# High digit's one-hot from eight shifted copies of the digit and four comparisons of 2048 elements, in place of four copies and eight comparisons of 1024

## The reference

```python
s0 = jnp.einsum('bshq,eq->bshe', _l2norm(q0), _l2norm(keys0))
s1 = jnp.einsum('bshq,eq->bshe', _l2norm(q1), _l2norm(keys1))
sc0, ix0 = jax.lax.top_k(s0, K)
sc1, ix1 = jax.lax.top_k(s1, K)
cs = (sc0[..., :, None] + sc1[..., None, :]).reshape(b, s, H, K * K)
ci = (ix0[..., :, None] + ix1[..., None, :]).reshape(b, s, H, K * K)
fs, pos = jax.lax.top_k(cs, K)
fi = jnp.take_along_axis(ci, pos, axis=-1)
w = jax.nn.softmax(fs, axis=-1)
down = expert_down[fi]
up = expert_up[fi]
inner = jnp.einsum('bsd,bshkd->bshk', hidden_states, down)
act = jax.nn.gelu(inner, approximate=False)
out = jnp.einsum('bshk,bshko->bso', act * w, up)
```

## Time and profile before

| | |
|---|---|
| time of three runs | 1363.95, 1364.64, 1365.32 us; median 1364.64 |
| profiled execution | 1364.77 us; its span 1363.0 us |
| DVE busy | 1241.4 us (91%) |
| PE busy | 1012.5 us (74%) |
| POOL busy | 925.8 us (68%) |
| ACT busy | 901.4 us (66%) |
| granted TensorE clock, mean | 0.76 |

### The profile page before, as it was taken

One profiled execution on the slowest core, in us unless ns is written; L12 is line 12 of the kernel. 1 busy time (PEld: TensorE's weight loads), 2 busy tenths in 40 slices (PEclk: granted clock), 3 DMA queues, 4 the chain that ended last, 5 costly groups with the idle time before them and its releaser, 6 DMA issues.

```text
span 1363.0 us, 38569 instructions
## 1 busy us (share of the span) xinstructions
PE 1012.5 (74%) x9443; PEld 659.5 (48%) x9443; DVE 1241.4 (91%) x9666; ACT 901.4 (66%) x4045; POOL 925.8 (68%) x1881
## 2 busy tenths in 40 slices
PE   2746777877878877887888788788867878877644
PEld 1514454645445554644555464455635545453433
DVE  4529696999999999999999999999999999999994
ACT  1546857577686867768686776868577686857442
POOL 4336666685868768586876858677685867768561
PEclk8867777679787786878777787877688787776665
DMA  2010000000000000000000000000000000000000
GB/s 56 7 28 3 9 13 10 11 13 11 14 3 23 4 13 13 12 13 4 23 5 13 13 12 13 4 23 4 13 13 11 13 4 17 4 8 13 6 6 7
DMA packets 35682, 16.56 MB, mean 12 GB/s; under 512 B 15392, under 2 KB 35248, under 8 KB 35458
## 3 DMA queue, kind: packets, MB, share of 16 engines
q1 hardware_dynamic: 34834, 13.81, 4.2%
q10 hardware_dynamic: 624, 0.30, 0.1%
HBM read 7.58 MB, written 6.01 MB: 10 GB/s over the span
## 4 chain that ended last, share of the span: by engine, by line
DVE 49%; ACT 13%; PE 12%; POOL 12%; issue 10%; SPq 1%; DMA 1%; DVEq 0%; POOLq 0%; ACTq 0%
DVE idx L1549 12%; DVE val L1547 7%; DVE scores L1552 6%; DVE oh L1562 6%; DVE cr L1620 6%; PE banks L1135 3%; DVE best L1618 3%; DVE wl L1582 3%; ACT ns_junk L942 3%; DVE masked L1502 2%; ACT act_g L919 2%; ACT eh L997 2%; POOL ce L691 2%; POOL std L654 2%; PE bankQ L1236 2%
## 5 line engine op out<-in xcount | busy, mean ns | idle before, releaser
L1549 DVE FIND_INDEX8 idx<-val,scores 128x8 uint16<-128x64 f32 x1472 | 298.0, 242 | 0.1
L1547 DVE MAX8 val<-scores 128x8 f32<-128x64 f32 x1472 | 205.6, 230 | 0.2
L1300 PE MATMUL bankM<-wl,oh 128*128 128x16 f16 x5888 | 161.0, 172 | 56.4 <-DVE wl L1582 52.4
L665 POOL TENSOR_TENSOR qscale<-nmx,power 128x16 f32<-128x16 f32 x46 | 151.1, 3284 | 60.9 <-DVE nmx L1526 60.9
L1300 PEld LDWEIGHTS bankM<-wl,oh 128*128 128x128 f16 x5888 | 157.1, 101 | 71.6 <-DVE wl L1582 61.6
L1552 DVE MATCH_REPLACE8 scores<-val,scores 128x64 f32<-128x64 f32 x736 | 149.6, 233 | 0.0
L1562 DVE TENSOR_SCALAR oh<-eh 128x1024 f16<-128x1024 int16 x368 | 134.1, 429 | 12.6 <-ACT eh L997 12.3
L1549 DVE MATCH_VALUE_LOAD idx<-val,scores 128x8 f32 x1472 | 140.2, 95 | 0.0
L942 ACT ACTIVATE ns_junk<-bankQ 128x32 f32<-128x32 f32 x736 | 132.8, 269 | 5.2 <-PE bankQ L1253 5.1
L942 ACT ACTIVATION_READ_ACCUMULATOR ns_junk<-bankQ 128x1 f32 x736 | 133.1, 282 | 0.0
L979 ACT ACTIVATE wcell<-wn 128x400 f16<-128x400 f32 x46 | 24.9, 542 | 136.6 <-POOL wn L716 136.6
(11 more groups left out here) (199 smaller groups left out, 3033.5 us busy)
## 6 DMA issues: line engine op xcount, KB each, us to landing
h_in<-h_rows SPq DMA_DIRECT2D x45, 64.0 KB, 2.7
out<-o_sb SPq DMA_DIRECT2D x45, 64.0 KB, 1.5
x_in<-in_x SPq DMA_DIRECT2D x16, 93.8 KB
x_in<-in_x SPq DMA_DIRECT2D x16, 62.5 KB
h_rows<-hsum SPq DMA_DIRECT2D x16, 62.0 KB
h_rows<-hsum SPq DMA_DIRECT2D x16, 61.0 KB
h_rows<-hsum SPq DMA_DIRECT2D x16, 60.5 KB
x_in<-in_x SPq DMA_DIRECT2D x16, 31.0 KB
```

The source lines that it names most:

```text
L665: g.tensor_tensor(qscale[c.slot(t)][:, :, :].rearrange("p h s -> p (h s)"), nmx[:, :, :].rearrange("p h s -> p (h s)"), power[0:QT, 0, :], ...
L1300: last = e.matmul(coef[:, g, :, :], oh[:, k, g, :, :].rearrange("p v t -> p (v t)"), wl[:, part, k, :, TG * g:TG * (g + 1)], start=k + par ...
L1547: last = v.max(out=v_[:, hd, s, best8], in_=src[:, hd, s, :])
L1549: last = v.max_index(out=i_[:, hd, s, best8], in_max=v_[:, hd, s, best8], in_values=src[:, hd, s, :])
```

## The change

`SHIFTS` is 8 in place of 4, and `VALUES`, the values of each copy, is 4 in place of 8.

```diff
@@ -20,7 +20,7 @@
 PAIRS = H // 2
 SLOTS = 32
 EH, EL, TG = 32, 4, 4
-SHIFTS = 4
+SHIFTS = 8
 VALUES = EH // SHIFTS
 QT = 128
 NQ = -(-B * T // QT)
```

## The result

| | before | after |
|---|---|---|
| median of the runs | 1364.88 us (1363.95 to 1365.32) | 1402.47 us (1401.38 to 1403.95) |
| profiled execution, its span | 1364.77, 1363.0 us | 1403.95, 1402.2 us |
| DVE, ACT busy | 1241.4, 901.4 us | 1229.6, 964.1 us |
| granted TensorE clock, mean | 0.76 | 0.766 |

The change makes the kernel slower: 1402.47 / 1364.88 = 1.0278, 95% interval 1.0266 to 1.0291. That is 37.6 us where 44 were forecast, and inside the range.

What follows compares the result with a forecast made beforehand. The prediction took the chain of waits, half DVE and half the other engines, as the bound. To 1364.8 us it added 43 for fourteen batches and 1.2 for the end, giving 1409 us, range 1385 to 1426.

Steps and rivals of the forecast that it cites:

- What bounds the kernel: Whole kernel: DVE has 49% of the chain, other engines the rest; about 20 of 46 copy sets lie on it.
- The price of a copy: On ACT: copies start 0.36 us apart, so four more cost 1.43 us a tile, 66 us in all.
- The saving on DVE: Comparisons: four of 2048 replacing eight save a fixed part of 0.065 us each, 0.26 a tile, 12 us in all.
- The batch's walk: Delay followed from tile 1 to the next tile 1: 3.1 us a batch, 43 us over fourteen three-tile batches.
- the sign that the walk gave for being wrong: On ACT: the walk is wrong if tile 2's copies come less than 1 us late.
- The other sign: On POOL: the walk is wrong if idle time at `nmx` or the next batch's squares shrinks with the delay.
- The first two batches: At the start: these batches have two tiles and more reserve, so nothing was counted for them.
- the term forecast for the end: Last tile's end, with no other work: 1.43 - 0.26 = 1.2 us added.
- The floor: Rival: only the 20 copy sets on the old chain count, less 7 us from comparisons: 1387 us; chance 0.2.
- The ceiling: Rival: all copies count in full, 66 us, and the comparisons give nothing back: 1431 us; chance 0.08.
- Faster: Rival: DVE sets the pace, ACT has room, and only the 12 us saved on DVE show: 1353 us; chance 0.05.
- No change: Rival: tile 2's reserve and DVE's gain eat the floor's 29 us, or the TensorE clock is granted higher; chance 0.04.

Runs made afterwards that it cites:

- dve_alone: The changed kernel with only the first four copies written per tile, the others zeroed once at the start, four comparisons of 2048 kept: 1352.92 us, ratio 0.9915.
- act_alone: The kernel before with four more copies per tile into a buffer nothing reads, ahead of the comparisons' signal; eight comparisons of 1024 stay: 1423.67 us, ratio 1.0438.
- many_t01: The kernel before with eight copies and four comparisons of 2048 in tiles 0 and 1, tile 2 as before: 1401.21 us, ratio 1.0276.
- many_t0: The kernel before with eight copies and four comparisons of 2048 in tile 0 of each batch alone: 1393.61 us, ratio 1.0214.
- spare_ahead: The kernel before with four copy-long activations on ACT in tile 0 alone, behind `wm` and ahead of convT, the norms and `hn`: 1395.08 us, ratio 1.0224.
- shifts2: The kernel before with two copies and sixteen comparisons of 512 per tile, in place of four and eight: 1394.83 us, ratio 1.0223.
- spare_behind: The kernel before with four copy-long activations on ACT in tile 0 alone, between `hn` and `hnT`: 1373.57 us, ratio 1.0064.
- act_behind: The kernel before with four copy-long activations on ACT behind `wm` in every tile, behind all three signals of `merged_weights`: 1383.97 us, ratio 1.0143.
- many_t1: The kernel before with eight copies and four comparisons of 2048 in tile 1 of each batch alone: 1377.57 us, ratio 1.0103.
- many_t2: The kernel before with eight copies and four comparisons of 2048 in tile 2 of each batch alone: 1365.44 us, ratio 1.0010.
- later4: The kernel before with tile 0's `merged_weights` behind `hn` on ACT, its DVE users behind two steps of tile 1's choosing, four copies: 1421.94 us, ratio 1.0418.
- later8: The same move as later4, with eight copies and four comparisons per tile: 1433.07 us, ratio 1.0498 against the kernel before.
- the kernels of the table: The kernel before, the changed kernel, and many_t2, many_t1, many_t0 and many_t01, with eight copies in some tiles only: medians 1364.88 to 1402.47 us.
- the two halves of the change: act_alone, the added copies without larger comparisons (+59.3 us), and dve_alone, the larger comparisons without added copies (-11.4 us).

## Why the prediction was right, and where its terms were off

**What bounds the kernel.** Right: the chain is shared by engines in the kernel before, and DVE's 96% did not hide the copies. dve_alone (-11.4) and act_alone (+59.3) show both sides of it.

**The price of a copy.** Right: 1.43 us for four, by the timeline. ACT's busy time rose by 62.7 us rather than 66.

**The saving on DVE.** Right: a mean of 697 ns, starts 0.60 apart, 11.8 us less busy, 11.4 us in dve_alone. By the distance of the starts the fixed part is 0.067, where 0.065 was forecast. The groups' busy time gives (134.1 - 120.4) / 184 = 0.074, as some comparisons of the kernel before take longer than 429 ns (six take some 0.6). The start of some 150 cycles that the Trainium skill gives every instruction ("VectorE: DVE Perf Modes", "Side-by-side: where the cycles go for N=2048 bf16"), with 29 us to gain, is not what the engine spends: the measured 11.8 decides.

**The batch's walk.** Right in its mechanism: ACT's copies went onto the chain in each batch, and the path led over tile 2's comparisons, PE, tile 0's copies, `hn` and the queries. Its size was off. It gave 3.1 us a batch, 43 over fourteen, and a batch costs 81.9 - 79.6 = 2.3.

The terms by tile: tile 2's copies were charged 1.43 less a reserve of 1.23, and all of 1.43 in every third batch. That reserve was spent in each batch (DVE begins 0.03 us after the last of them), but POOL's shorter `qscale` gave back more than what was left of the delay, where the walk had POOL take it over in full. With tiles 0 and 1 the time is +37.0, with all three +37.6. Tile 1 cost 13.4 / 16 = 0.84 a tile rather than 1.2, and tile 0 29.4 / 16 = 1.84 rather than 1.43.

The walk followed one batch, and a batch of the kernel before is not like the next one. From tile 1's first copy to tile 2's it took the 24.81 us of that batch; in the next one it is 26.00, and the mean of eleven is 25.55. After the change it is 26.00 each time. So the sign that the walk gave for being wrong, tile 2's copies less than 1 us late, came (0.46) by the mean and did not (1.19) by the batch followed. The other sign did not come: POOL's idle time at `nmx` went from 60.9 to 62.7 us and at the squares from 29.1 to 38.5.

**Luck in the size.** The distance of 81.9 is not the mark of this change. The changed kernel, many_t01, many_t0, spare_ahead and shifts2 all have it on average, from the third interval at the latest, with 12, 8 or 4 further activations a batch, or with DVE's work added in their place. In the changed kernel and many_t01 the granted clock falls and rises at the same places of every batch, in many_t0 and spare_ahead at the same places of every second one. That the clock's pattern holds the batches there is argued from this, not shown. If it is so, a walk that adds delays can't give the 2.3, and that it came within 0.8 of it is partly luck.

**The theory of two rounds.** The expectations rest on a later theory: the distance of the batches is the longer of two closed paths, A over the copies of all three tiles and B over tile 1's and tile 0's copies and VectorE between. It met many_t01 (1400 to 1407, measured 1401) and spare_behind (1372, measured 1374); spare_ahead was expected by many_t0's time (1385 to 1394, measured 1395). It missed act_alone by 13 us, act_behind by 18, many_t1 by 6, many_t0 by 9, many_t2 by 4, dve_alone by 4, shifts2 by 19, later4 by 71 and later8 by 44. So it is not a model of this kernel.

**The first two batches.** I counted nothing for them, for their reserve, and this step failed. In the timeline of DVE the tiles of those batches, and the first of three tiles, begin their comparisons at these times, before:

```profile
138.79 1.43 DVE L1562 TENSOR_SCALAR oh<-eh 128x1024 f16<-128x1024 int16 x4
...
163.38 1.44 DVE L1562 TENSOR_SCALAR oh<-eh 128x1024 f16<-128x1024 int16 x4 [2.57 <-ACT eh L997]
...
232.41 1.43 DVE L1562 TENSOR_SCALAR oh<-eh 128x1024 f16<-128x1024 int16 x4 [3.10 <-ACT eh L997]
...
276.79 1.42 DVE L1562 TENSOR_SCALAR oh<-eh 128x1024 f16<-128x1024 int16 x4
```

and after:

```profile
141.45 1.28 DVE L1562 TENSOR_SCALAR oh<-eh 128x2048 f16<-128x2048 int16 x2
...
168.97 1.30 DVE L1562 TENSOR_SCALAR oh<-eh 128x2048 f16<-128x2048 int16 x2 [4.46 <-ACT eh L997]
...
241.46 1.29 DVE L1562 TENSOR_SCALAR oh<-eh 128x2048 f16<-128x2048 int16 x2 [4.74 <-ACT eh L997]
...
285.60 1.29 DVE L1562 TENSOR_SCALAR oh<-eh 128x2048 f16<-128x2048 int16 x2
```

The delay is 2.7, 5.6, 9.1 and 8.8 us (6.3 in the tile left out after the second). DVE waited for the copies there already (2.57 and 3.10), and waits longer now. 2.0 us of it were there ahead of the first copy (137.10 after, 135.13 before). They are hardly the change's: in the kernels of the table the first copy begins at 134.8 to 137.3.

The sum as measured: 8.8 up to 276.79; then to the comparisons at 1284.2, which are at 1322.2 now, another 29.2 in 12.7 batches, 2.3 each; and a rest of 1.2, the term forecast for the end. That is 39.2, the difference of the two spans; the medians are 37.6 apart. So the forecast of 44 was near because too much a batch and too little at the start partly cancelled, which is luck as well.

**The rivals.** The floor (1387) fell: its 20 sets became 44, since a later ACT puts more of its copies on the chain. Its sentence that no reserve can bring it lower was not put to the test, as the time came out above. The ceiling (1431) fell, though what it was said to need came: tile 2's reserve was spent every time. Faster (1353) is what dve_alone shows, and would have needed copies at no cost. No change fell, and the mean granted clock hardly moved (0.76 and 0.766). Of the signs in the profile, DVE's idle time ahead of the comparisons (35.9 us, forecast some 40), the copies' share of the chain (9%, forecast 4% or more) and the mean of a comparison (697 ns) came as told.

**What stays open.** The parts don't add. Tiles 0 and 1 alone are 29.4 + 13.4 = 42.8, together 37.0; the two halves of the change are 47.9 together, 37.6 as one. And act_behind costs 10.5 us less than spare_ahead, which is a part of it. The share of TensorE in this is argued, not shown. The granted clock differs between the same products at the same place of a batch. By stretches (PE, PEld busy; clock, DMA share, GB/s) the rows of the convolution, L1135, are, before:

```profile
587.36:591.80 4.44, 4.44 (x10) 2.11 (x10) 0.76 0.05 15
667.06:670.90 3.84, 3.84 (x10) 1.81 (x10) 0.87 0.07 19
746.60:749.96 3.36, 3.36 (x10) 1.54 (x9) 1.00 0.11 27
```

and after:

```profile
685.94:690.10 4.16, 4.16 (x10) 1.97 (x10) 0.82 0.06 16
767.88:772.03 4.15, 4.15 (x10) 1.97 (x10) 0.82 0.06 18
```

Before, the stretch is at the full 2.4 GHz in one batch of three and partly at 1.2 in the others; after, it is the same in both. In act_alone's chain the same ten take 5.44 us at 691.07, and that kernel's mean clock is lower, 0.744 to 0.750 in its four runs against 0.755 to 0.764 in the kernel before. Work on the path thus costs a few tenths more or less a batch (up to 1.1 us within this row), by where the clock's change falls among it. An edit that moves the batch by 2 us moves that too. No run held the clock fixed, so how much of the 10 us that the sum of the halves is off comes from it is not settled. Nor is why tile 0's copies cost more than their 1.43, beyond that their kernel, too, runs at 81.9 us a batch.

## What to carry to other kernels

A busy share (66% for ACT here) is no reserve: ask whether the instructions lie on the chain of waits, and what stands behind them in their engine's order. Four activations in tile 0 cost 30 us ahead of `hn` and 9 behind it, at the same occupancy. Price added work as the distance of starts times the passes of the chain, and expect more passes once that engine is late. Before you take the time of one edit as its price, run it together with others and look at the distance of the batches: here five kernels share 81.9 us, and one edit costs 10 us less than a part of it. Joining vector instructions saves only a fixed part each (0.07 us here), so of two, four and eight copies four is best, with 2.2% lost at two and 2.8% at eight.

## What the runs showed that I had not expected

The busy time of a group is not its fixed parts alone: with sixteen comparisons of 512 a tile, 11 of the 35.7 us more are one comparison in tile 0 that takes 1.08 us, beside POOL's `h`. The starts give 0.07 us for an instruction at both steps. The same ten products of the convolution take 3.36 us at a granted clock of 1.00 and 4.44 at 0.76 (5.44 in act_alone). Single edits don't add to within 10 us of 1400, and the distance of the batches stays at 81.9 us over edits as unlike as four further activations in one tile and two copies in place of four.
